# A graph network's softmax pass: four of sixteen edge columns looked up by matmul, and the running sums made one scan

## The reference

```python
z = x @ Wn
e = edge_attr @ We
s_src = (z @ att_src)[src]
s_dst = (z @ att_dst)[dst]
s_edge = e @ att_edge
score = jax.nn.leaky_relu(s_src + s_dst + s_edge, negative_slope=0.2)
max_per = jnp.maximum(jax.ops.segment_max(score, dst, num_segments=n), NEG)
score_exp = jnp.exp(score - max_per[dst])
denom = jax.ops.segment_sum(score_exp, dst, num_segments=n)
alpha = score_exp / (denom[dst] + 1e-08)
msg = (z[src] + e) * alpha[:, None]
out = jax.ops.segment_sum(msg, dst, num_segments=n)
```

## Time and profile before

| | us |
|---|---|
| median of 3 runs (15794.82 to 15804.54) | 15800.14 |
| the profiled execution | 15804.67 |
| its span (first to last instruction) | 15802.9 |

### The profile page before, as it was taken

One profiled execution on the slowest core, in us unless ns is written; L12 is line 12 of the kernel. 1 busy time (PEld: TensorE's weight loads), 2 busy tenths in 40 slices (PEclk: granted clock), 3 DMA queues, 4 the chain that ended last, 5 costly groups with the idle time before them and its releaser, 6 DMA issues. The chain is left out here.

```text
span 15802.9 us, 183580 instructions
## 1 busy us (share of the span) xinstructions
PE 7374.6 (47%) x51805; PEld 6150.3 (39%) x51805; DVE 8542.6 (54%) x21162; ACT 2292.7 (15%) x6525; POOL 10874.9 (69%) x10916
## 2 busy tenths in 40 slices
PE   3444445444443333333333455886887999200001
PEld 3444444444433333333333114886885555100000
DVE  3555554444444444444444895665665776344443
ACT  1222222222210000000000231111111111000000
POOL 4777776777767777777777202776776777577775
PEclk9999955555555555555555565998998999555555
DMA  1222222333323333333333672211221222122221
GB/s 61 71 71 72 72 69 86 101 101 101 101 81 96 97 93 97 93 97 93 97 93 96 236 272 91 44 43 37 44 44 37 49 49 42 43 65 65 65 65 48
DMA packets 615795, 1294.05 MB, mean 82 GB/s; under 512 B 221540, under 2 KB 342825, under 8 KB 589494
## 3 DMA queue, kind: packets, MB, share of 16 engines
q0 software_dynamic: 350336, 469.63, 13.9%
q1 hardware_dynamic: 251300, 765.30, 13.8%
q10 hardware_dynamic: 14112, 58.61, 1.0%
HBM read 623.08 MB, written 669.64 MB: 82 GB/s over the span
## 5 line engine op out<-in xcount | busy, mean ns | idle before, releaser
L517 POOL DMA_INDIRECT rows<-spline_table,index x3136 | 3209.2, 1023 | 1198.4 <-issue 1002.7
L851 POOL DMA_INDIRECT rows<-gcn_table,index x2548 | 2506.7, 984 | 1008.9 <-issue 719.5
L891 PE MATMUL p_slots<-part,one_lo 128*128 128x208 bf16 (+1 forms) x25872 | 2972.3, 277 | 444.3 <-DVE one_lo L909 443.9
L891 PEld LDWEIGHTS p_slots<-part,one_lo 128*128 128x128 bf16 x25872 | 2371.1, 98 | 1045.0 <-DVE one_lo L909 487.8
L1141 PE MATMUL a_p_label<-tw,a_label 8*128 8x64 f32 x3136 | 1040.6, 433 | 2710.5 <-DMA a_label_row<-in_label_rows 2710.5
L1085 POOL DMA_INDIRECT sent<-a_msg,a_place x1568 | 1629.5, 1039 | 477.7 <-issue 477.4
L1141 PEld LDWEIGHTS a_p_label<-tw,a_label 8*128 8x128 f32 x3136 | 844.4, 327 | 2718.5 <-issue 2718.5
L1427 POOL DMA_INDIRECT e_rows<-soft_table,e_index x1568 | 1525.5, 973 | 516.4 <-issue 471.2
L1077 POOL DMA_INDIRECT a_rows<-att_table,a_index x1568 | 1489.6, 950 | 484.9 <-issue 477.4
L672 DVE TENSOR_TENSOR msg<-rows,weight 128x1024 f32<-128x1024 f32 x196 | 241.4, 1232 | 1887.0 <-DMA rows<-spline_table,index 1887.0
L1173 DVE TENSOR_TENSOR a_product<-a_rows,a_xdst 128x1024 f32<-128x1024 f32 x98 | 120.1, 1226 | 2074.1 <-DMA a_rows<-att_table,a_index 2074.1
(11 more groups left out here) (398 smaller groups left out, 15401.3 us busy)
## 6 DMA issues: line engine op xcount, KB each, us to landing
running_dst<-a_run SPq DMA_DIRECT2D x98, 1600.0 KB
running_src<-s_run SPq DMA_DIRECT2D x98, 1600.0 KB
running<-e_run SPq DMA_DIRECT2D x98, 656.0 KB, 3.0
s_rows<-sent ACTq DMA_DIRECT2D x98, 584.0 KB, 7.0
keys<-key_rows SPq DMA_DIRECT2D x200, 256.0 KB, 3.3
running<-run SPq DMA_DIRECT2D x98, 520.0 KB
rows<-spline_table,index POOLq DMA_INDIRECT x3136
running<-run SPq DMA_DIRECT2D x98, 512.0 KB
```

The source lines that it names most:

```text
L517: pool.indirect_dma_start(out=rows[h][:, k, :], out_offset=None, in_=table, in_offset=offsets(index[h][:, k:k + 1])).then_inc(gathered[h], 16)
L851: pool.indirect_dma_start(out=rows[h][:, K + k, :], out_offset=None, in_=table, in_offset=offsets(index[h][:, k:k + 1])).then_inc(gathered ...
L891: ins = nc.tensor.matmul(to, one_lo[h][:, q, e:e + P], flat(part[:, q, :, :]), start=q == 0 and part_no == 0, stop=q == CLASSES - 1 and pa ...
```

## The change

In `softmax_pass`, K = 4 of the 16 columns of a block are looked up on PE, and POOL gathers the other 12. The slots are split into 7 classes of 7 (49 = 7 x 7), each row has Z = 65 values, so one matmul has 65 x 7 = 455 columns, and a block has 4 x 7 x 3 = 84 of them. The tile `e_p_slots` holds two columns for each of two groups. The message has its 16 edges innermost, one step adds the sum that comes in from the block before, and one scan over 81 x 16 values takes the place of the 16 steps. The scan's factors (`carried`) and the copy back to edge rows (`run_rows`) are new on ScalarE, which counts `copied`. SP's store, and the attribute loads behind it, wait for `copied`.

Outside the pass: the wide keys are made (five VectorE operations over 1,568 values, then `turn_keys`) at the end of the first layer, between `node_ranges` and the layer norm. `split_wide` makes the three parts beside `spread_to_edges`. A few tiles of the first layer get a shorter life. Some fills are larger.

```diff
+WIDE_CLASSES = 7
+WIDE_CLASS = J // WIDE_CLASSES
...
+def split_wide(nc, rows, rest, parts, step):
+    left = rows
+    for k, part in enumerate(parts):
+        of = left.rearrange("p (q s) c -> p q c s", s=WIDE_CLASS)
+        step(nc.vector.tensor_copy(part[:], of))
+        if k + 1 < len(parts):
+            step(nc.vector.tensor_tensor(rest[:].rearrange("p (q s) c -> p q c s", s=WIDE_CLASS), of, part[:], ALU.subtract))
+            left = rest[:]
...
+    S, W, Z = C + 1 + EDIM, C + 2 + EDIM, C + 1
+    K = 4
+    GATHERED = B - K
+    GROUPS = [slice(0, K // 2), slice(K // 2, K)]
+    FIRST_MADE, ONE_HOTS = 1, 1 + WIDE_CLASSES
+    SECOND_MADE = ONE_HOTS + 8
+    SCORED = SECOND_MADE + 8
+    MADE = SCORED + 1
+    per = MADE + 4
...
             def store(h, i):
-                sp.wait_ge(stepped, INIT + per * (2 * i + h + 1))
-                sp.dma_start(running_v[:, bass.ds((2 * i + h) * B, B), :], run[h][:]).then_inc(stored[h], 16)
+                n = 2 * i + h
+                sp.wait_ge(stepped, INIT + per * (n - 1) + ONE_HOTS)
+                load_keys(h, n + 2)
+                sp.wait_ge(copied, n + 3)
+                sp.dma_start(running_v[:, bass.ds(n * B, B), :], run_rows[h][:]).then_inc(stored[h], 16)
...
             with act.Fori(0, IT) as i:
                 for h in range(2):
                     n = 2 * i + h
-                    act.wait_ge(stepped, INIT + per * n)
-                    stage(1 - h, (n + 1) * B)
+                    act.wait_ge(gathered[h], 16 * GATHERED * (i + 1))
+                    stage_index(h, (n + 2) * B)
                     act.wait_ge(stepped, INIT + per * n + SCORED)
                     nc.scalar.activation(factor[h][:], exps[h][:], ACT.Exp).then_inc(activated, 1)
-                    act.wait_ge(gathered[h], 16 * B * (i + 1))
-                    stage_index(h, (n + 2) * B)
+                    act.wait_ge(activated, 2 * n + 1)
+                    nc.scalar.activation(carried[:, :, 1:B], repeat(factor[h][:, B + 1:2 * B], S), ACT.Copy).then_inc(activated, 1)
+                    act.wait_ge(stepped, INIT + per * (n + 1))
+                    act.wait_ge(stored[h], 16 * (i + 1))
+                    nc.scalar.activation(run_rows[h][:, :, 0:S], run[h][:].rearrange("p c b -> p b c"), ACT.Copy)
+                    nc.scalar.activation(run_rows[h][:, :, S], top[h][:, 1:1 + B], ACT.Copy).then_inc(copied, 1)
+                    stage(h, (n + 2) * B)
...
+            def multiply(h, g):
+                for k in range(K // 2):
+                    e = (g * (K // 2) + k) * P
+                    for q in range(WIDE_CLASSES):
+                        for part_no, part in enumerate(parts):
+                            ins = nc.tensor.matmul(p_slots[g][:, k, 0:Z * WIDE_CLASS], one_lo[h][:, q, e:e + P], flat(part[:, q, :, :]),
...
+                    pe.wait_ge(stepped, INIT + per * (n - 1) + ONE_HOTS)
                     pe.wait_ge(loaded[h], 16 * (B // PACK) * (i + 1))
-                    pe.wait_ge(stepped, INIT + per * (2 * i + h - 1))
                     for g in range(B // PACK):
                         ins = nc.tensor.transpose(flat(attr[h][:, g * PACK:(g + 1) * PACK, :]), attr_t[h][:, g, :], sig["ident"][:])
                     ins.then_inc(turned, 1)
+                    multiply(h, 0)
+
+                    pe.wait_ge(stepped, INIT + per * (n - 1) + SECOND_MADE)
+                    multiply(h, 1)
...
-                    step(nc.vector.tensor_tensor(msg[h][:, :, 0:C], rows[h][:, :, 0:C], spread(factor[h][:, 0:B], C), ALU.mult))
+                    step(nc.vector.tensor_tensor(msg[h][:, 0:C, :], by_column(rows[h][:, :, 0:C]), repeat(factor[h][:, 0:B], C), ALU.mult))
                     assert done[0] == MADE
+                    step(nc.vector.tensor_tensor(msg[h][:, C + 1:S, :], by_column(attr[h]), repeat(factor[h][:, 0:B], EDIM), ALU.mult))
+                    step(nc.vector.tensor_copy(msg[h][:, C, :], factor[h][:, 0:B]))
+                    after()
+                    step(nc.vector.scalar_tensor_tensor(msg[h][:, :, 0], run[1 - h][:, :, B - 1], factor[h][:, B:B + 1], msg[h][:, :, 0], ALU.mult, ALU.add))
+
+                    dve.wait_ge(activated, 2 * n + 2)
+                    dve.wait_ge(copied, n + 1)
+                    after()
+                    step(nc.vector.tensor_tensor_scan(flat(run[h][:]), flat(carried[:]), flat(msg[h][:]), 0.0, ALU.mult, ALU.add))
...
+                                step(V.tensor_scalar(in_class[:], src_hi[:, 0:T], -float(WIDE_CLASS // 2), 1.0 / WIDE_CLASS, ALU.add, ALU.mult))
+                                step(V.tensor_scalar(in_class[:], in_class[:], ROUND, None, ALU.add))
+                                step(V.tensor_scalar(in_class[:], in_class[:], -ROUND, None, ALU.add))
+                                step(V.scalar_tensor_tensor(wide_slot[:, 0:T], in_class[:], -float(WIDE_CLASS), src_hi[:, 0:T], ALU.mult, ALU.add))
+                                step(V.scalar_tensor_tensor(wide_key[:], in_class[:], float(P), src_lo[:, 0:T], ALU.mult, ALU.add))
+
+                            on_vector(nc, sig, wide_keys, block)
+                            turn_keys(nc, sig, block, scope, wide_key, wide_key_rows)
                             layer_norm(nc, sig, y, xs, block, scope, mean_and_own)
```

More of the change, by code:

```diff
@@ L1425, in _ @@
                     pool.sem_inc(sig["rounds"].sem, 1)
-                    for k in range(B):
-                        pool.indirect_dma_start(out=rows[h][:, k, :], out_offset=None, in_=table,
+                    for k in range(GATHERED):
+                        pool.indirect_dma_start(out=rows[h][:, K + k, :], out_offset=None, in_=table,
                                                 in_offset=offsets(index[h][:, k:k + 1])).then_inc(gathered[h], 16)
@@ L1432, in stage_index @@
             def stage_index(h, at):
-                nc.scalar.copy(index[h][:], edge["src"][:, bass.ds(at, B)]).then_inc(indexed[h], 1)
+                nc.scalar.copy(index[h][:], edge["src"][:, bass.ds(at + K, GATHERED)]).then_inc(indexed[h], 1)
             def stage(h, at):
+                nc.scalar.activation(slot[h][:], edge["src_slot"][:, bass.ds(at, K)], ACT.Copy)
                 nc.scalar.activation(keep[h][:], edge["keep"][:, bass.ds(at, B)], ACT.Copy)
                 nc.scalar.activation(at_dst[h][:], edge["at_dst"][:, bass.ds(at, B)], ACT.Copy).then_inc(staged[h], 1)
-            stage_index(0, 0)
-            stage_index(1, B)
-            stage(0, 0)
+            act.sem_inc(copied, 2)
+            for h in range(2):
+                stage_index(h, h * B)
+                stage(h, h * B)
             with act.Fori(0, IT) as i:
@@ L1470, in _, with after, pick, gather @@
+            one_slots(0, lambda ins: ins.then_inc(stepped, per - ONE_HOTS))
             with dve.Fori(0, IT) as i:
                 for h in range(2):
[L1472 removed]
+                    n, done = 2 * i + h, [0]
                     def step(ins):
                         ins.then_inc(stepped, 1)
[L1476 to L1482 removed]
+                        done[0] += 1
+                    def after(back=0, at=None):
+                        dve.wait_ge(stepped, INIT + per * n + (done[0] - back if at is None else at))
+                    def pick(g):
+                        slots = p_slots[g][:, :, 0:Z * WIDE_CLASS].rearrange("p k (c s) -> p k c s", s=WIDE_CLASS)
+                        mask = one_hi[h][:, GROUPS[g], :].unsqueeze(2).broadcast_to([P, K // 2, Z, WIDE_CLASS])
+                        step(nc.vector.tensor_tensor(picked[g][:], slots, mask, ALU.mult))
+                    def gather(g):
+                        step(nc.vector.tensor_reduce(rows[h][:, GROUPS[g], 0:Z], picked[g][:], AX.X, ALU.add))
+                    def by_column(t):
+                        return t.rearrange("p b c -> p c b")
+                    dve.wait_ge(looked, 2 * n + 1)
+                    after()
+                    pick(0)
+                    assert done[0] == FIRST_MADE
+                    dve.wait_ge(spread_keys[1 - h], 16 * (i + 1 + h))
+                    one_hots(1 - h, step)
+                    assert done[0] == ONE_HOTS
+                    dve.wait_ge(staged[1 - h], i + 1 + h)
+                    one_slots(1 - h, step)
+                    after(at=FIRST_MADE)
+                    gather(0)
@@ L1516, in _ @@
-                    step(nc.vector.tensor_copy(msg[h][:, :, C], factor[h][:, 0:B]))
-                    dve.wait_ge(stored[h], 16 * i + 16 * (h == 0))
-                    for k in range(B):
-                        before = run[h][:, k - 1, 0:S] if k else run[1 - h][:, B - 1, 0:S]
-                        after()
-                        step(nc.vector.scalar_tensor_tensor(run[h][:, k, 0:S], before, factor[h][:, B + k:B + k + 1], msg[h][:, k, :], ALU.mult, ALU.add))
-                    step(nc.vector.tensor_copy(run[h][:, :, S], top[h][:, 1:1 + B]))
```

118 lines of the change are left out of this document (75 added, 43 removed).

## The result

| | before | after |
|---|---|---|
| median, us (4 runs each, same chip) | 15799.74 (15794.82 to 15804.54) | 15621.9 (15617.89 to 15627.07) |
| span of the profiled execution, us | 15802.9 | 15616.2 |
| first message to last message of the softmax pass, 97 blocks, us | 2006.1, or 20.68 a block | 1801.4, or 18.57 a block |

The ratio is 0.9887, with a 95% interval of 0.9875 to 0.9899. The change gains 178 us. The forecast was 326 us, so 148 are missing, and the time lies 2 us above the range. The sign was right.

A forecast was written before the change was run, and what follows sets the result against it. POOL's endless gathers were taken as today's bound, the attribute-load wait as the new one at 17.15 us a block. 15,804.67 - 335 (pass) + 9 (outside) = 15,478.7 profiled, given as 15,474 us; range 15,400 to 15,620.

The forecast's parts named there:

- Part 1: POOL in the softmax pass: 12 gathers for 16 at 1.30 us each, 15.6 us a block.
- the attribute chain: Softmax pass, closed chain over two blocks: matmuls 16.6, mask to scan end 9.9, copy and load 7.8; 17.15 us a block.
- The rival that came true: POOL stays the bound as gathers rise above 1.30 us under VectorE's one-hots; 1.72 cancels the gain; chance 0.01.
- The reason against it: Window with rows of 16: POOL busy 150.62 us for 152 instructions, under 1.0 each, against gathers reaching 1.72.
- Part 2: PE in the softmax pass: 84 matmuls of 192 ns, 16.1 us, plus transposes and waits: 16.6 us a block.
- PE alone: Rival: PE sets the softmax pass's pace because loads land in time; 16.6 us a block, 15,421 us; chance 0.20.
- Part 3: VectorE in one softmax block: 5.7 us to the edge's score, 9.9 from second masking to scan end; 15.6 us.
- Part 4: New wait for `copied`: attribute loads behind SP's store start transposes 7.8 us after the scan's end; 17.15 us a block.
- Part 5: Start and end of the softmax pass: first scan ends at 35 us, 5 for last copy and store; 1,704 us.
- Part 6: Outside the pass: wide keys and late square root cost 9 us in the norm; the 28.5 us split hides.
- The clock: Rival: PE's granted clock stays low; slower than before below a mean of 0.80, 16,985 us at 0.50; chance 0.04.

The follow-up runs named there:

- the fastest kernel: Changed kernel with message factor in PSUM, key and attribute loads ahead of the store, split subtracts in seven pieces, scan in three: 15396.1 us, ratio 0.9747.

## Why the prediction was wrong

- **Part 1, the step that failed.** "12 x 1.30 = 15.6 us a block" took the length of a gather as a property of the gather. It depends on what VectorE does beside it. The true term was 12 x 1.247 + 3.6 = 18.6, above PE and the attribute chain, so the bound never left POOL.
- **The rival that came true was the one with a chance of 0.01**, that POOL stays the bound because a gather gets dearer. It named one-hots, which held nothing in this pass (0.94 us beside them; in the graph pass with rows of 32 it was up to 1.08, rows below), and it was priced only at a full loss of the gain (1.72 us a gather). A part of that, 1.55 with its pause, was enough to halve the gain. The reason against it was a window in which VectorE's two-input multiply is 0.59 us long, too short to hold much. That window's 150.62 us for 152 gathers are 0.99 each, already above 0.94. The change made such instructions of 2.07 and 2.86 us; the rows to read were in the softmax pass itself.

```profile
12610.17 1.41 DVE L909 TENSOR_SCALAR one_lo<-keys,lanes 128x768 bf16<-128x768 f16 x4
12610.33 1.07 POOL L851 DMA_INDIRECT rows<-gcn_table,index  x1 [0.30 <-issue]
```

- **Part 2, right.** 192 ns a matmul forecast, 195 measured; 16.6 us a block forecast for PE alone, 16.43 measured once it was the bound.
- **Part 3, right in sum.** Scan 2.86 forecast and measured, message 1.96 and 2.07, attributes' message 0.5 and 0.417. In the fastest kernel VectorE waits for PE 1.1 us of the 16.42, which leaves 15.3 for 15.6. The strided read of PSUM cost nothing (416 ns before, 417 after). What I made of the line sizes in the Trainium skill, "SBUF — State Buffer", section "Door 1: The DMA port swizzle", that it would add 0.05 us, is not borne out.
- **Part 4, right in size, wrong in rank.** 7.8 us from scan to transposes forecast, 7.4 measured, and the wait for `e_attr_t` is there with 140 us. But it had POOL's slack to hide in. With the 16 steps, and POOL out of the way, loads moved and split in pieces gained 37 us together (15463.54 to 15426.42; 25 by the ratios, 0.9783 and 0.9767), of which the split is some 6.
- **Part 5, right.** 35 us from the start of the pass to the first scan's end forecast, 33.6 measured (13609.84 to 13643.48).
- **Part 6, half right.** 9 us in the norm forecast, 8.9 measured. The split's length was right, but "hides with over 4 us left" asked only when VectorE is done, and not what it does to POOL on the way: 10 us.
- **The clock** was no danger, but not the 1.00 that I said the profile would show: 0.97 in the pass, with short falls after PE's idle time.

The two misses are one: 138 us in the blocks and 10 at the split, both by holds.

## What to carry to other kernels

Ahead of merging many short VectorE instructions into a long one, look at what GpSimd does beside it. If GpSimd's indirect DMAs are the bound, an instruction of VectorE with two SBUF inputs can cost nearly its own length on GpSimd's path (2.0 us for 2.29, 2.45 for 2.86), however idle VectorE is. Put one input into PSUM, or cut the instruction into pieces: both gave over 100 us here for next to no VectorE time. And read the spread of a group beside its mean: one gather in sixteen at 1.30 us or more for 0.94 was the sign beforehand.

## What the runs showed of the hardware

- A gather that starts while VectorE runs a long instruction with two SBUF inputs (2.07, 2.29, 2.86 and 6.13 us here) ends 0.75 to 0.83 us after that instruction; one that is already under way when it starts is not held (14507.01; in the changed kernel's pass 96 gathers that began 0.05 to 0.87 us ahead of the message took 0.94 to 0.97). It gets through between two instructions that follow each other at once. With one input in PSUM, no hold (0.94 to 0.96 us beside 2.07 and 2.28). Beside steps of 0.31 us a gather takes 1.02 us at most.
- A fast `tensor_scalar` with one SBUF input (0.60 ns a value) holds as well (1.83 us); a cast at 1.80 ns a value does not, nor do this pass's one-hot rows at 0.64, while those of the graph pass (12610.17) held for 0.13 us. What tells them apart is open.
- The granted clock fell when PE had sat idle 2.0 us (0.57 over the next 4 us, then 1.00): 84 matmuls took 18.05 us for 16.37. After 0.41 us idle they took 16.37.
